# A third pair of score banks, with four seeded chunks and the rounding ahead of the seed, in a graph layer on one Trainium2 core

## The reference

```
z   = leaky_relu(lap_mul(A, x) @ W1 + b1)           # lap_mul(A, x) = d * (A @ (d * x)), d = 1/sqrt(rowsum A)
d2  = sq[:, None] + sq[None, :] - 2 * z @ z.T       # sq = sum of squares of each row of z
S   = exp(-sqrt(max(d2, 0) + 1e-10) / 2)
S   = where(rank in its row < 4, S, 0)              # only the four nearest of each row stay
out = lap_mul(S + A, x) @ W2 + b2
return layernorm(x + out)
```

## Time and profile before

| | us |
|---|---|
| median of 3 runs | 2832.22 (2832.13 to 2835.3) |
| the profiled execution | 2839.99 |
| its span in the profile | 2838.1 |
| TensorE busy | 2545.1 (90%) |
| VectorE busy | 2408.6 (85%) |
| ScalarE busy | 1582.5 (56%) |
| GpSimd busy | 980.0 (35%) |

### The profile page before, as it was taken

How to read it: one execution, slowest core, us unless ns; L and a number is a source line. 1 busy time by engine, 2 the same in 40 slices (tenths; PEclk the granted TensorE clock), 3 DMA queues, 4 the chain that set the end, 5 groups by cost and what they waited for, 6 DMA issues and landing times.

```text
span 2838.1 us, 28440 instructions
## 1 busy us (share of the span) xinstructions
PE 2545.1 (90%) x9592; PEld 1780.5 (63%) x9592; DVE 2408.6 (85%) x1667; ACT 1582.5 (56%) x1806; POOL 980.0 (35%) x708
## 2 busy tenths in 40 slices
PE   1477999999899998889999999999999997998898
PEld 0133444444577776568778787878778775466665
DVE  7988898876788887999999999998999977288887
ACT  0000000001377767679989898988989884266764
POOL 0000000000000000016566565656666675667770
PEclk9688999999999999999999999999999998999999
DMA  9999999995788850014455554554454669999996
GB/s 385 422 398 377 386 421 421 421 403 204 293 317 332 333 198 30 0 60 141 141 153 143 150 151 143 144 155 140 131 158 141 174 179 408 378 362 327 356 351 227
DMA packets 144632, 713.43 MB, mean 251 GB/s; under 512 B 18624, under 2 KB 26560, under 8 KB 82560
## 3 DMA queue, kind: packets, MB, share of 16 engines
q1 hardware_dynamic: 123072, 669.71, 62.9%
q0 software_dynamic: 16832, 33.84, 5.0%
q10 hardware_dynamic: 4608, 8.39, 0.8%
HBM read 679.62 MB, written 32.24 MB: 251 GB/s over the span
## 4 chain that ended last, share of the span: by engine, by line
PE 56%; DVE 19%; DMA 10%; ACT 7%; issue 5%; POOL 2%; SPq 1%; DVEq 0%; ACTq 0%
PE PS L571 14%; DVE R L1216 6%; PE PS L661 5%; PE PS L662 5%; PE PS L663 5%; DVE R L1222 5%; DMA cache<-at 5%; DMA ring<-at 4%; PE PS L749 3%; PE PS L703 3%; PE PS L694 3%; PE PS L695 3%; DVE al_t L1295 3%; PE PS L631 3%; PE PS L665 3%
## 5 line engine op out<-in xcount | busy, mean ns | idle before, releaser
L1025 POOL TENSOR_TENSOR al<-ring,ah 128x1024 fp32r<-128x1024 f32 x252 | 605.8, 2410 | 432.3 <-ACT ah L878 432.2
L1216 DVE MAX8 R<-R 128x8 f32<-128x8192 f32 x64 | 556.2, 8691 | 91.9 <-ACT R L910 89.5
L910 ACT ACTIVATE R<-PS 128x1024 f32<-128x1024 f32 x512 | 523.0, 1022 | 183.9 <-PE PS L663 107.8
L1222 DVE FIND_INDEX8 R<-R,R 128x8 uint32<-128x8192 f32 x64 | 555.9, 8685 | 0.0
L661 PE MATMUL PS<-zh,zst 128*128 128x512 f32 x1024 | 413.9, 404 | 64.5 <-ACT PS L895 57.0
L1010 POOL CAST zst<-zh 128x128 fp32r<-128x128 f32 (+1 forms) x64 | 28.0, 438 | 1217.2 <-DVE zl L1168 878.6
L662 PE MATMUL PS<-zl,zst 128*128 128x512 f32 x1024 | 404.0, 395 | 0.0
L663 PE MATMUL PS<-zh,zst 128*128 128x512 f32 x1024 | 403.9, 394 | 0.0
L571 PE MATMUL PS<-cache,R 128*128 128x512 f32 x680 | 309.7, 611 | 29.9 <-DVE R L1114 15.9
L1071 POOL DMA_INDIRECT R<-xs_dram,R x256 | 269.5, 1053 | 118.2 <-issue 81.1
L661 PEld LDWEIGHTS PS<-zh,zst 128*128 128x128 f32 x1024 | 195.3, 191 | 133.8 <-ACT PS L895 71.5
(11 more groups left out here) (149 smaller groups left out, 4174.0 us busy)
## 6 DMA issues: line engine op xcount, KB each, us to landing
R<-at SPq DMA_DIRECT2D x151, 1024.0 KB, 7.9
ring<-at SPq DMA_DIRECT2D x144, 1024.0 KB, 6.9
ring<-at SPq DMA_DIRECT2D x252, 512.0 KB, 3.9
cache<-at SPq DMA_DIRECT2D x125, 1024.0 KB, 18.3
raw_sq<-at SPq DMA_DIRECT2D x22, 1024.0 KB, 7.5
raw_z<-at SPq DMA_DIRECT2D x21, 1024.0 KB, 7.7
raw_ring<-at SPq DMA_DIRECT2D x21, 1024.0 KB
acc_dram<-R POOLq DMA_DIRECT2D x63, 256.0 KB, 5.7
```

Of the source, the lines that this page charges most:

```text
L910: act.activation(score[j % 2][:, c * EC:(c + 1) * EC], PS[:, 2 * (c % 2):2 * (c % 2) + 2].rearrange("p b c -> p (b c)"), ACT.Copy).then_in ...
L1025: pool.tensor_tensor(al[:, k % SPLIT], raw[k % RAW], ah[:, k % SPLIT].bitcast(F32), ALU.subtract)\
L1216: v.max(top[:, j], score[j % 2]).then_inc(dve3, 1)
L1222: v.max_index(place[:, j], top[:, j], score[j % 2]).then_inc(placed, 1)
```

## The change

- Three pairs of score banks (0-1, 2-3, 6-7): chunk c uses pair c % 3, except in the very first tile. The accumulators of the pieces have two banks (4, 5) instead of three.
- The seeded chunks are 4, 5, 6, 7 instead of 0, 2, 4, 6. The seed of chunk c + 3 is written in slot c (slots 1 to 4).
- In a slot ScalarE does: copy c, round the next piece, seed c + 3, flush.
- `round_piece` no longer waits for `prodb` (the whole piece two before), but for `ah_read` (its first four matmuls) and `rest` (GpSimd has read ah). `rest_of_piece` now itself waits for `prodb`.

```diff
-RAW, SPLIT = 3, 2
+RAW, SPLIT, BANKS = 3, 2, 2
+SEEDED = (4, 5, 6, 7)
...
-            return c % 2 == 0 and not (first and j == 0)
+            return c in SEEDED and not (first and j == 0)
+        def pair(first, j, c):
+            k = c % 2 if first and j == 0 else c % 3
+            return PS[:, (0, 2, 6)[k]:(0, 2, 6)[k] + 2]
... (scores)
+                if first and j == 1 and c == 0:
+                    pe.wait_ge(sq_row_ok, len(SEEDED))
                 if on_seed:
-                    pe.wait_ge(seeded, NE // 2 * (GT * g + j) + c // 2 + 1 - NE // 2)
-                elif not (first and j == 0 and c < 2):
-                    pe.wait_ge(copied, NE * (GT * g + j) + c - 1)
+                    pe.wait_ge(seeded, len(SEEDED) * (GT * g + j - 1) + SEEDED.index(c) + 1)
+                elif not (first and j == 0):
+                    pe.wait_ge(copied, NE * (GT * g + j) + (c - 2 if c >= 3 else (-1, 0, -2)[c]))
+                elif c >= 2:
+                    pe.wait_ge(copied, c - 1)
... (squares_row)
-                if i < 2:
-                    pe.wait_ge(copied, NE - 1 + i)
+                c = SEEDED[i]
+                before = [k for k in range(i) if SEEDED[k] % 3 == c % 3]
+                if before:
+                    pe.wait_ge(sq_row_ok, before[-1] + 1)
                 else:
-                    pe.wait_ge(sq_row_ok, i - 1)
+                    pe.wait_ge(copied, NE)
... (piece)
-                bank = PS[:, 4 + ib % 3]
+                bank = PS[:, 4 + ib % BANKS]
...
-                        pe.wait_ge(flushed, HB * g + ib - 2)
+                        pe.wait_ge(flushed, HB * g + max(ib - BANKS + 1, 0))
...
-                    pe.matmul(bank, xgl[:, t], ah[:, s, kk], start=False, stop=False)
+                    i = pe.matmul(bank, xgl[:, t], ah[:, s, kk], start=False, stop=False)
+                i.then_inc(ah_read, 1)
... (round_piece)
-                    act.wait_ge(prodb, n - SPLIT + 1)
+                    act.wait_ge(ah_read, n - SPLIT + 1)
+                    act.wait_ge(rest, n - SPLIT + 1)
... (group_act)
-                            act.wait_ge(sq_row_ok, NE // 2)
-                            seed(0)
-                        if c % 2 == 0 and not (first and j == 0) and (c < NE - 2 or not (is_last(g) and j == GT - 1)):
-                            act.wait_ge(copied, NE * (GT * g + j) + c + 1)
-                            seed((c // 2 + 1) % (NE // 2))
+                            act.wait_ge(sq_row_ok, len(SEEDED))
...
                             if has_next(g, back, k):
                                 round_piece(g - back, k + 1)
+                        if c + 3 in SEEDED and not (first and j == 0):
+                            act.wait_ge(copied, NE * (GT * g + j) + c + 1)
+                            seed(c + 3)
+                        for back, k in pieces_at(g, j, c):
                             if k % PIECES == 0 and not (isinstance(g, int) and g == back and k == 0):
                                 flush_unit(*((g - back, k // PIECES - 1) if k else (g - back - 1, HB - 1)))
... (rest_of_piece)
+                if not (isinstance(g, int) and n < SPLIT):
+                    pool.wait_ge(prodb, n - SPLIT + 1)
+                    hold(pool)
                 pool.wait_ge(rounded, n + 1)
```

More of the change, by code:

```diff
@@ L214, in build @@
         acc = R2[:, 0:HB * BC]
-        sq_row = R2[:, 0:NE // 2 * EC]
-        at_ = [HB * BC]
+        sq_row = {c: R2[:, i * EC:(i + 1) * EC].rearrange("p (b c) -> p b c", b=2) for i, c in enumerate(SEEDED)}
+        at_ = [max(HB * BC, len(SEEDED) * EC)]
         def cut(n):
@@ L702, in second_half @@
                 for kk in range(PT):
-                    i = pe.matmul(PS[:, 4 + ib % 3], xgh[:, p * PT + kk], al[:, s, kk], start=False,
+                    i = pe.matmul(PS[:, 4 + ib % BANKS], xgh[:, p * PT + kk], al[:, s, kk], start=False,
                                   stop=p == PIECES - 1 and kk == PT - 1)
@@ L720, in group_pe @@
                         if is_first(g) and (j, c) == (0, NE - 1):
-                            for i in range(NE // 2):
+                            for i in range(len(SEEDED)):
                                 squares_row(i)
```

27 lines of the change are left out of this document (12 added, 15 removed).

## The result

The changed kernel takes 2829.97 us (median of 12 runs, 2826.49 to 2834.17) where the kernel before takes 2835.01 on the same chip: ratio 0.9983, 95% interval 0.9976 to 0.9991. That is 5 us faster, where 2809 was forecast, and outside the range of 2799 to 2827.

What follows compares the result with a forecast made beforehand. VectorE was taken to bound a group up to tile 2 and TensorE from tile 3, with the loss at the swap. 5 x 3.8 + 2.0 + 1.5 + 1.0 = 23.5 us off gave 2809 us, range 2799 to 2827.

Steps and rivals of the forecast that it cites:

- The third pair at the swap: Tile 3, where the bound passes from VectorE to TensorE: 12 matmuls move into TensorE's 4.5 us stall; 3.8 us a group.
- small waits for seeds: Tiles 0 and 1: TensorE loses some 2.4 us, in waits that a third pair mostly removes.
- Two accumulators: the flush of two units back lies four pieces, some 13 us, ahead. 0.: Accumulator banks of the pieces: the flush comes early enough for two banks; cost 0.
- The clock: Behind the stall in tile 3: half clock loses 2.45 us a group; gain 4.6 if it stays up, 2.7 if not.
- Rounding released earlier ... Cost 0: ScalarE waits for less, GpSimd for `prodb`, with a slot to spare; cost 0, or TensorE held up to 1 us.
- Group 0: VectorE-bound group with a late tile 1: seeds no longer stand between chunks; gain 1.5 us, bounds 1.3 to 2.9.
- Group 1: Swap without a clock fall: 2.72 us gained less 0.7 for ScalarE's catch-up, so 2.0 us.
- Group 7: TensorE's stall there is on a rounding, which comes one seed earlier; gain 1.0 us, bounds 0 and 2.
- Tiles 4 to 7 at TensorE's pace, 19.5 us: Tiles behind the swap: TensorE without gaps, 19.5 us per tile still; seeds in four slots running cost 0.
- A: Rival: TensorE's new lead ends at a piece not yet rounded, leaving 1 us per group; 2824 us, chance 0.10.
- C: Rival: bunched seeds come late for chunks 5 to 7 in TensorE-bound tiles; slower, 2840 at 0.9 us each; chance 0.07.
- B: Rival: ScalarE becomes the bound behind the swap; gain under 0.8 us a group, 2827 to 2832 us, chance 0.11.

Runs made afterwards that it cites:

- e7: Changed kernel with the ninth accumulator's flush moved from slot 3 to slot 1 of tile 2, and pieces of tiles 0 and 1 in even slots; ratio 0.9928.
- e12: Changed kernel with the ninth accumulator's flush in slot 1 of tile 2, and two GpSimd waits until VectorE is past its small operations; ratio 0.9925.
- e1: Changed kernel with the flush of a group's ninth accumulator moved from slot 3 to slot 1 of tile 2; ratio 0.9942.
- e2: Changed kernel with GpSimd's subtraction cut to a quarter of its columns, leaving low halves of A wrong; ratio 0.9947.
- e9: Changed kernel with both the ninth accumulator's flush in slot 1 of tile 2 and GpSimd's subtraction cut to a quarter; ratio 0.9885.
- e4: Kernel before with two accumulators instead of three and nothing else; ratio 0.9972.
- e14: Changed kernel with the old release: the rounding waits for `prodb`, GpSimd for nothing of its own; ratio 0.9979.
- e10: Changed kernel with the ninth accumulator's flush in slot 1 of tile 2, and each GpSimd subtraction split into four of 256 columns; ratio 0.9937.
- e15: e7 with one more GpSimd wait, for VectorE's index copy, before its subtraction in slot 6 of tile 0; ratio 0.9938 against the kernel before.
- e3: Kernel before with GpSimd's subtraction cut to a quarter of its columns, leaving low halves of A wrong; ratio 0.9959.
- e13: Kernel before with the new order and release alone: two pairs, even chunks seeded, three accumulators; ratio 0.9998.

## Why the prediction was wrong

The forecast was faster by 23.5 us, and it is 5. Two steps failed, both put at nothing: the two accumulators, and what GpSimd's subtractions do to VectorE. Point by point:

- **The third pair at the swap** (groups 2 to 6, 3.8 us each, bounds 2.2 to 4.9): the mechanism was right. With the seam's stall out of the way tile 1 to 7 goes from 115.57 to 110.9 us (e7, e12), 4.7 a group, next to the prediction's own 4.6 for a clock that stays up. It does stay up there, so the 3.8, chosen for a half clock in one group of two, was too careful. In the changed kernel itself it was 2.8. One reading under it was wrong: the "small waits for seeds" of some 2.4 us in tiles 0 and 1 are not in the earlier trace rows, where line 661 waits 4.9 us in the group and 4.5 of them are the stall.
- **"Two accumulators: the flush of two units back lies four pieces, some 13 us, ahead. 0."**: the step that failed first. It holds inside a group. At the group's seam nine units, an odd number, meet two banks, and the flush stands in the same slot, fourth on ScalarE. 4.0 us of stall in each of groups 2 to 7; it cost 9.1 us with the held time in place (e1) and 23.5 without it (e2 to e9, 1.6 of that by chance in group 0). In the kernel before, the same two banks cost nothing (e4), because there the old stall went for the new one.
- **The clock**: the half clock was expected behind a shorter stall in tile 3, if at all. It followed the stall to tile 2, still 27.2 us of it in place of 34.0.
- **No term for the seam of VectorE**: the step that failed second, and it is missing in the prediction altogether. "Rounding released earlier ... Cost 0" looked only at who waits for GpSimd by semaphore. I didn't ask whose short operations run beside its 2.4 us. The sign stood in the trace of before: line 1266 took 3.30 us in groups 2 on and 1.23 in group 1, the same instruction (the row below: shortest, median and longest in ns). Cost 2.7 us at each of six seams, 16.3 us, and gave 0.7 back at tile 0 to 1 (line 1266 no longer caught, 2.1; line 1262 caught, 1.4). The earlier release itself did not do it (e14). The part's other bound, TensorE held for up to 1 us in few slots, came as 1.25 us in six groups, during VectorE's tile 0, and cost nothing there.

  The line of that instruction in the kernel before, all seven of it:

```profile
L1266 DVE TENSOR_TENSOR R<-R,tiny x7: 1226/3302/3371, 1253.7 to 2210.2; 128x1024 f32<-128x1024 f32 x7
```

- **Group 0**: forecast 1.5, bounds 1.3 to 2.9; tile 0 to 1 went from 22.54 to 19.57, 3.0 us, just above the upper bound. The half clock at the start, kept in the forecast, was gone in this execution (e2 and e10 have it, and take 21.13), so that much is luck. **Group 1**: 2.0 forecast, 1.2 measured. **Group 7**: 1.0 forecast, 0.1 measured, because it has the seam's stall as well; in e12 it was 1.6 (tile 1 to 7, 123.62 to 122.04).
- **Tiles 4 to 7 at TensorE's pace, 19.5 us**: right, and rivals A and C didn't show: TensorE waits for a seed only during VectorE's tile 0, 0.7 us in each of groups 2 to 7, and not in these tiles. A's stall at a rounding showed once the seam's was gone, with up to 2.6 us in e1 and 1.2 in e7, as the restart that the forecast itself had worked out. B's 2827 to 2832 holds the measured time, but ScalarE didn't bound the tiles.

The sum as it happened: 3.0 (group 0) + 1.2 (group 1) + 14.0 (groups 2 to 6, tile 1 to 7) + 0.1 (group 7) + 4.1 (tile 0 to 1, six times) - 16.3 (the seam) = 6.1 us of stage, and 5.0 of the median time. The terms that were forecast at 23.5 came to 18.3, and the held time, which had no term, took 12.2 on balance.

What would have shown it, of the prediction's own list: VectorE without a wait before tile 3, yes; a TensorE stall that ends at a rounding in tile 3, no, it ended at a flush in tile 2. Its group length of 156 us was 159.4, which says that something is wrong and not where. The list named no row at the seam, so the held time had no place on it.

## What to carry to other kernels

When buffers that rotate are cut from three to two, check the wrap: count modulo the new number across the loop's end, and see how far in front of the first reuse the release is written. Before costing a shift of one engine against another, look in the trace for one instruction with two durations: here the longer one showed a neighbour in the way, and the shift decided anew which operations were caught. And before a small gain is read as "the idea doesn't work", take the suspected causes out together as well as one by one, because each may hide the other.

## What the hardware showed

- A VectorE operation of 0.17 to 0.19 us lasted up to 2.4 us when it began within a GpSimd subtraction of 2.4 us on 128x1024 elements. Caught were TENSOR_TENSOR and TENSOR_SCALAR, down to 8 elements a partition, and COPY of 32. In the score stages of all sixteen traces, every one of the 204 operations of these three kinds that began over 0.3 us before the end of a running subtraction, whatever its length, was held until that end. TENSOR_REDUCE (0.19), MAX8 and FIND_INDEX8 (8.7) weren't, nor did RECIPROCAL last longer (0.18 at 1557.03 in e15, inside a subtraction from 1555.40 to 1557.80). It goes the other way too: GpSimd's cast took 1.28 us instead of 0.28 beside line 1266.
- Busy time holds waiting: VectorE shows 11 us more of it with the same instructions, so a busier engine isn't a sign of more work.
- Behind each of the six idles of TensorE of 3.9 to 4.0 us in the changed kernel the granted clock fell to 0.50, for 3.4 or for 6.8 us from one group to the next. The length of an idle alone did not decide it: full clock followed idles of 2.12 us (e1, group 2) and 3.10 (e3, group 2), and half clock followed 1.84 (the changed kernel, group 0, at 1193.46), 1.98 (e13, group 2) and 2.7 to 2.8 (e4, all six groups). I found nothing in the rows that tells the 3.4 from the 6.8.
